# Two mixture-of-experts FFNs: blocks of 32 rows on four 32-column tiles in place of blocks of 64 on two

## The reference

```
x   = layernorm(h)
p   = softmax of the two largest of (x @ gate)
y_e = (silu(x @ W1_e) * (x @ W3_e)) @ W2_e        # hidden width 512 in the first FFN, 1024 in the second
out = h + sum over the two chosen experts of p_e * y_e
```

## Time and profile before

| | |
|---|---|
| median of 3 runs | 972.81 us (970.16 to 972.89) |
| profiled execution | 968.8 us, its span 967.1 us |
| busy over the span | PE 802.5, PEld 461.0, DVE 477.5, ACT 407.9, POOL 219.5 us |
| granted TensorE clock, mean | 0.894 |
| router and steps of the first FFN | about 384 to 548 us of the span |
| router and steps of the second FFN | about 673 to 951 us |

### The profile page before, as it was taken

How to read it: one execution, slowest core, us unless ns; L and a number is a source line. 1 busy time by engine, 2 the same in 40 slices (tenths; PEclk the granted TensorE clock), 3 DMA queues, 4 the chain that set the end, 5 groups by cost and what they waited for, 6 DMA issues and landing times. The chain is left out here.

```text
span 967.1 us, 15054 instructions
## 1 busy us (share of the span) xinstructions
PE 802.5 (83%) x4860; PEld 461.0 (48%) x4861; DVE 477.5 (49%) x1186; ACT 407.9 (42%) x589; POOL 219.5 (23%) x276
## 2 busy tenths in 40 slices
PE   3859548899997897499999397886599999999993
PEld 1857426533663455454444164554444444444441
DVE  4975443399767672733333367563622222222332
ACT  4133125543244555244555043444255555555541
POOL 1051000277020100123343121332112222222110
PEclk8579757999989999699999798799599999999996
DMA  3000055000034320611111334870603103700004
GB/s 115 1 0 1 0 175 228 1 0 1 1 97 128 101 56 3 230 34 43 43 43 33 104 111 142 241 219 4 234 12 122 53 22 128 308 22 22 25 12 136
DMA packets 52953, 78.62 MB, mean 81 GB/s; under 512 B 9796, under 2 KB 45764, under 8 KB 49700
## 3 DMA queue, kind: packets, MB, share of 16 engines
q1 hardware_dynamic: 48040, 67.37, 21.2%
q0 software_dynamic: 4864, 10.63, 3.6%
HBM read 54.77 MB, written 10.49 MB: 67 GB/s over the span
## 5 line engine op out<-in xcount | busy, mean ns | idle before, releaser
L2195 PE MATMUL psum<-ring,f_x_t 128*64 x480 | 218.8, 598 | 1.2 <-DVE f_x_t L1971 1.2
L2197 PE MATMUL psum<-f_w_up,f_x_t 128*64 128x512 f32 x480 | 218.8, 598 | 0.0
L2073 ACT ACTIVATE f_w_up<-ring 128x1024 f32 x120 | 125.7, 1050 | 44.0 <-issue 44.0
L2195 PEld LDWEIGHTS psum<-ring,f_x_t 128*64 128x64 f32 x480 | 60.8, 136 | 114.3 <-issue 114.3
L2213 PE MATMUL psum<-ring,f_gated_t 128*64 x480 | 113.5, 379 | 1.7 <-issue 1.7
L1966 DVE TENSOR_TENSOR f_gated<-f_silu,psum 128x512 f32<-128x512 f32 x60 | 41.2, 687 | 148.9 <-PE psum L2197 148.9
L2215 PE MATMUL psum<-f_w_down,f_gated_t 128*64 128x256 f32 x480 | 113.5, 379 | 0.0
L2056 ACT ACTIVATE f_gated_t<-psum 128x512 f32<-128x512 f32 x60 | 35.8, 597 | 140.0 <-PE psum L2204 140.0
L2213 PEld LDWEIGHTS psum<-ring,f_gated_t 128*64 128x64 f32 x480 | 65.6, 137 | 61.3 <-issue 35.3
L1983 DVE COPY f_w_down<-ring 128x1024 f32 x60 | 42.1, 701 | 48.0 <-PE psum L2215 23.1
L2215 PEld LDWEIGHTS psum<-f_w_down,f_gated_t 128*64 128x64 f32 x480 | 65.6, 137 | 0.0
(11 more groups left out here) (297 smaller groups left out, 1422.9 us busy)
## 6 DMA issues: line engine op xcount, KB each, us to landing
ring<-in_f_experts SPq DMA_DIRECT2D x24, 1536.0 KB, 7.3
a_stack_q<-a_parts SPq DMA_DIRECT2D x96, 64.0 KB, 2.0
a_stack_k<-a_parts SPq DMA_DIRECT2D x96, 64.0 KB, 2.0
rows_in<-h SPq DMA_DIRECT2D x4, 1024.0 KB, 12.7
ring<-rows_out SPq DMA_DIRECT2D x8, 512.0 KB, 5.4
ring<-in_a_wqkv SPq DMA_DIRECT2D x2, 768.0 KB, 4.4
x_in<-in_x SPq DMA_DIRECT2D x1, 1024.0 KB, 4.8
out<-x SPq DMA_DIRECT2D x4, 256.0 KB, 2.1
```

The lines of the kernel that those rows point to most:

```text
L2073: act.activation(w_up[:, b, CT * CHUNK * side:CT * CHUNK * (side + 1)], k.ring[:, bass.ds(at + start, CT * CHUNK)], ACT.Copy).then_inc(s_w ...
L2195: pe.matmul(psum[0:HALF, 2 * b + side, :], x_t[:, xb, t, 0:HALF], k.ring[:, bass.ds(at + (CHUNK_COLS * c + start), CHUNK)], start=(t == 0) ...
L2197: last = pe.matmul(psum[HALF:P, 2 * b + side, :], x_t[:, xb, t, HALF:P], w_up[:, b, start:start + CHUNK], start=(t == 0), stop=(t == CT - 1))
```

## The change

An expert now owns blocks of 32 rows, and a step works on four of them, on four tiles of 32 columns. MAXBLK becomes 18. The first tile still reads `ring`; the other three read copies. VectorE copies the up weights of tiles 1 and 2 (2048 columns each, one instruction) and the down weights of tile 1; ScalarE copies the up weights of tile 3 and the down weights of tiles 2 and 3. The copies for tile 3 lie in `x1` and `h`, which are free by then. The engines' lists are written anew around these copies, and VectorE and ScalarE load ring columns for two tiles at once (`ring_columns`). `over`, `in_block` and `past` become views of `w_down`, and the router's constants are widened. The core of the diff:

```diff
-HALF = P // 2
-MAXBLK = ((2 * TOK + E * (HALF - 1)) // HALF + 1) // 2
+QUARTER = P // 4
+MAXBLK = ((2 * TOK + E * (QUARTER - 1)) // QUARTER + 3) // 4
...
-        past = sb("past", [P, 2 * PAIRED, E])
-        expert = sb("expert", [P, 3, 2 * PAIRED])
-        table = sb("table", [P, 2, PAIRED, 2], I32)
-        w_up = sb("w_up", [P, 2, 2 * CT * CHUNK])
-        w_down = sb("w_down", [P, 2, CHUNK // P * C])
+        expert = sb("expert", [P, 3, 4 * PAIRED])
+        table = sb("table", [P, 2, PAIRED, 4], I32)
+        own_up = sb("w_up", [P, 4, 2 * CT * CHUNK])
+        w_up = {(1, 0): own_up[:, 0], (1, 1): own_up[:, 1], (2, 0): own_up[:, 2], (2, 1): own_up[:, 3],
+                (3, 0): k.x1[:].rearrange("p t b n -> p (t b n)"), (3, 1): k.h[:].rearrange("p t b n -> p (t b n)")}
+        w_down = sb("w_down", [P, 3, 2, CHUNK // P * C])
...
 # VectorE
+            def copy_up(j, at, c, tile, b):
+
+                if chunks == 2 and tile == 1:
+                    loads = dve.value_load(table[0:1, 1, bass.ds(j, 1), 3:4], min_val=16, max_val=16 * E)
+                    dve.wait_ge(s_loaded[c], loads)
+                    dve.wait_ge(s_table, 1)
+                dve.tensor_copy(w_up[tile, b], k.ring[:, bass.ds(at[tile - 1] + CHUNK_COLS * c, 2 * CT * CHUNK)]).then_inc(s_uv, 1)
...
             dve.wait_ge(s_table, 1)
-            for c in range(chunks):
-                copy_down(0, c, c)
+            if chunks == 1:
+                dve.wait_ge(s_loaded[0], 16 * E)
+            at = ring_columns(0)
+            copy_up(0, at, 0, 1, 0)
+            copy_up(0, at, 0, 2, 0)
             take_x(0, 0)
-            gate(0, 0)
-            take_x(1, 1)
...
+            else:
+                ahead = ring_columns(1)
+                copy_up(1, ahead, 0, 1, 1)
+                take_x(1, 1)
+                copy_up(1, ahead, 0, 2, 1)
+                copy_down(0, at, 0, 0)
+                gate(0, 0)
 
-            def block_step(i, odd, more=True):
+            def block_step(i, odd, at, more=True):
                 j = 2 * i + (1 if odd else 2)
+                ahead = None
                 if chunks == 2:
-                    copy_down(j, 0, 0)
+                    copy_up(j, at, 1, 1, 1)
+                    copy_up(j, at, 1, 2, 1)
+                    copy_down(j, at, 0, 0)
                     gate(2 * j, 0)
                     take_y(j - 1, 1 - odd, 16 * i)
                     if more:
+                        ahead = ring_columns(j + 1)
+                        copy_up(j + 1, ahead, 0, 1, 0)
                         take_x(j + 1, 1 - odd)
-                    copy_down(j, 1, 1)
+                        copy_up(j + 1, ahead, 0, 2, 0)
+                    copy_down(j, at, 1, 1)
                     gate(2 * j + 1, 1)
                 else:
                     if more:
+                        ahead = ring_columns(j + 1)
+                        copy_up(j + 1, ahead, 0, 1, 1 - odd)
                         take_x(j + 1, 1 - odd)
-                    copy_down(j, 0, odd)
+                        copy_up(j + 1, ahead, 0, 2, 1 - odd)
+                    copy_down(j, at, 0, odd)
                     gate(j, odd)
                     take_y(j - 1, 1 - odd, 16 * i)
...
 # ScalarE, the same in both block_steps: take_gated, copy_up of tile 3, silu_of, copy_down
+            def copy_down(j, at, c, b):
...
+                for tile in (2, 3):
+                    act.activation(w_down[:, tile - 1, b, :],
+                                   k.ring[:, bass.ds(at[tile - 2] + (CHUNK_COLS * c + 2 * CT * CHUNK), CHUNK // P * C)],
+                                   ACT.Copy).then_inc(s_da, 1)
...
 # TensorE
             def up(q, xb, b, at, c):
+                pe.wait_ge(s_uv, 2 * q + 2)
+                pe.wait_ge(s_ua, q + 1)
+                pe.wait_ge(s_table, 1)
                 for side in range(2):
-                    pe.wait_ge(s_wu, 2 * q + side + 1)
                     for t in range(CT):
                         start = CHUNK * (CT * side + t)
-                        pe.matmul(psum[0:HALF, 2 * b + side, :], x_t[:, xb, t, 0:HALF],
-                                  k.ring[:, bass.ds(at + (CHUNK_COLS * c + start), CHUNK)], start=(t == 0), stop=(t == CT - 1))
-                        last = pe.matmul(psum[HALF:P, 2 * b + side, :], x_t[:, xb, t, HALF:P],
-                                         w_up[:, b, start:start + CHUNK], start=(t == 0), stop=(t == CT - 1))
+                        first, final = t == 0, t == CT - 1
+                        pe.matmul(psum[0:QUARTER, 2 * b + side, :], x_t[:, xb, t, 0:QUARTER],
+                                  k.ring[:, bass.ds(at + (CHUNK_COLS * c + start), CHUNK)], start=first, stop=final,
+                                  tile_position=(0, 0))
+                        for tile in range(1, 4):
+                            rows = slice(QUARTER * tile, QUARTER * tile + QUARTER)
+                            last = pe.matmul(psum[rows, 2 * b + side, :], x_t[:, xb, t, rows],
+                                             w_up[tile, b][:, start:start + CHUNK], start=first, stop=final,
+                                             tile_position=(0, QUARTER * tile))
                     last.then_inc(s_up, 1)
...
```

More of the change, by code:

```diff
@@ L1914, in _ @@
             dve.wait_ge(s_rank, 1)
-            step(dve.scalar_tensor_tensor(place[:], earlier_blocks[:].unsqueeze(1).broadcast_to(every), float(HALF),
+            step(dve.scalar_tensor_tensor(place[:], earlier_blocks[:].unsqueeze(1).broadcast_to(every), float(QUARTER),
                                           psum[:, 5, 0:TT * E].rearrange("p (t e) -> p t e", t=TT), ALU.mult, ALU.add))
@@ L2056, in take_gated @@
                 act.activation(gated_t[:, b, :], psum[:, G_BANK + b, :], ACT.Copy).then_inc(s_gto, 1)
-            def second_expert(j):
-                act.wait_ge(s_table, 1)
[L2061 to L2074, removed]
@@ L2076, in _, with ring_columns, copy_up @@
-            second = second_expert(0)
-            for side in range(2):
-                copy_up(second, 0, side, 0)
+            def ring_columns(j):
+                _, columns = nc.values_load_multi_w_load_instructions(
+                    table[0:1, 0, bass.ds(j, 1), 2:4], [mybir.EngineType.Activation], min_val=0,
+                    max_val=(RING_EXPERTS - 1) * chunks * CHUNK_COLS)
+                return columns
+            def copy_up(j, at, c, b):
+                if chunks == 2:
+                    loads = act.value_load(table[0:1, 1, bass.ds(j, 1), 3:4], min_val=16, max_val=16 * E)
+                    act.wait_ge(s_loaded[c], loads)
+                    act.wait_ge(s_table, 1)
+                act.activation(w_up[3, b], k.ring[:, bass.ds(at[1] + CHUNK_COLS * c, 2 * CT * CHUNK)], ACT.Copy).then_inc(s_ua, 1)
@@ L2079, in _ @@
+            act.wait_ge(s_table, 1)
+            act.wait_ge(s_nd, 32)
             if chunks == 1:
[L2080 to L2083, removed]
+                act.wait_ge(s_loaded[0], 16 * E)
+            at = ring_columns(0)
+            copy_up(0, at, 0, 0)
             if chunks == 2:
+                copy_up(0, at, 1, 1)
+                silu_of(0, 0)
+                copy_down(0, at, 0, 0)
@@ L2085, in _, with block_step @@
                 take_gated(0, 0)
-                second = second_expert(1)
-                copy_up(second, 0, 0, 0)
+                copy_up(1, ring_columns(1), 0, 0)
                 silu_of(1, 1)
-                copy_up(second, 0, 1, 0)
-            def block_step(i, odd, more=True):
+                copy_down(0, at, 1, 1)
+            else:
+                copy_up(1, ring_columns(1), 0, 1)
+                silu_of(0, 0)
+                copy_down(0, at, 0, 0)
+            def block_step(i, odd, at, more=True):
@@ L2103, in block_step @@
                     silu_of(2 * j + 1, 1)
-                    if more:
-                        copy_up(second, 0, 1, 0)
+                    copy_down(j, at, 1, 1)
                 else:
@@ L2108, in block_step, with turn @@
                     if more:
-                        second = second_expert(j + 1)
-                        copy_up(second, 0, 0, 1 - odd)
+                        ahead = ring_columns(j + 1)
+                        copy_up(j + 1, ahead, 0, 1 - odd)
                     silu_of(j, odd)
[L2112 to L2116, removed]
+                    copy_down(j, at, 0, odd)
+                return ahead
+            def turn(i):
+                block_step(i, 0, block_step(i, 1, ring_columns(2 * i + 1)))
+            turn(0)
             with act.Fori(1, PAIRS) as i:
-                block_step(i, 1)
-                block_step(i, 0)
-            block_step(PAIRS, 1, more=False)
+                turn(i)
+            block_step(PAIRS, 1, ring_columns(2 * PAIRS + 1), more=False)
             take_gated(chunks * MAXBLK - 1, 1)
```

111 lines of the change are left out of this document (68 added, 43 removed).

## The result

The changed kernel takes **975.12 us** (median of 12 runs, 971.43 to 980.68), the kernel before beside it 970.66 (12 runs, 968.39 to 973.33). The ratio is 1.0049, 95% interval 1.0026 to 1.0073: slower by half a per cent, where 955 was forecast. The profiled execution took 976.63 us, its span 974.6 (before: 968.8 and 967.1).

A forecast was written before the change was run, and what follows sets the result against it. TensorE was taken to bound the expert stages, as steps times its time per step. The sum -36.2 + 12 + 2.1 + 2.6 + 1 + 1 = -17.5, put on the median 972.81, gave 955.3 us; range 940 to 973.

The forecast's parts named there:

- Does a step keep its length?: Expert steps: four 32-column tiles replace two of 64, each streaming its own columns; taken as no loss.
- C: Up and down products: four tiles streaming 512 columns do not hold the pace; 989 or 1025 us, chance 0.07.
- D: TensorE's loop body, nearly doubled, is fetched again at every turn; 23 us, giving 979 us, chance 0.03.
- Fewer steps: Both FFNs: MAXBLK from 20 to 18 saves two steps of 12.01 us and two of 6.11, -36.2 us.
- The turn: TensorE's sequencer at loop turns and entry: branch and ring-column loads outlast queued matmuls; 6.0 us per FFN, +12 for both.
- VectorE's odd chunk: Second FFN: VectorE's queued copies make the gate 0 to 0.3 us late; +1 us over 18 steps.
- The queue ahead of the branch: TensorE's queue holds 16 to 18 matmuls, about four groups of down, covering 1.0 to 1.2 us instead of 2.5.
- Rival A: TensorE's loop turns: no stall, the queue stays far enough ahead; 943 us, chance 0.21.
- The first FFN: First FFN: later gate(0) at its start +2.6 us, TensorE's turns +6.0; VectorE's 4.7 us fit the 6.1 us step.
- B: VectorE's odd chunk in the second FFN, or GpSimd in the first, decides; 966 us, chance 0.14.
- Router: Router before both FFNs: longer block lists (`past` 320 to 576 elements, `over` 128 to 256) cost +2.1 us for both.
- E: Like the forecast, but several small terms at their ends, within 0.3% of before; 972 us, chance 0.05.

The follow-up runs named there:

- e1: Changed kernel with the second FFN's experts (weights and gate columns) stored in another order on the host: 951.53 us, ratio 0.9815 to the kernel before.
- e7: Kernel before the change, with only the same reordering of the second FFN's experts as e1: 971.06 us, ratio 1.0012.
- e5: Changed kernel with the four edits of e1, e2, e3 and e4 together: 935.9 us, ratio 0.9647 to the kernel before.
- e2: Changed kernel with TensorE's loop over pairs of steps written out in both FFNs: 972.42 us, ratio 1.0033 to the kernel before.
- e3: Changed kernel with VectorE's take_y moved later, behind reading ring columns (first FFN: also the first copy; first pair written out): 969.68 us, ratio 0.9999 to before.
- e4: Changed kernel with VectorE's take_x(1) moved behind the second copy, down copy and gate(0) at the first FFN's start: 973.8 us, ratio 1.004 to before.
- e9: e5 with VectorE's and ScalarE's loops over pairs of steps written out as well: 932.88 us, ratio 0.9636 to the kernel before.

## Why the prediction was wrong

**The step that failed** is "Does a step keep its length?". It asked only for the rate of four tiles and took "no loss" for the whole step. No term of the sum held the ring's refill: the size of the blocks moves an expert's last use and the next one's first use against the steps, while a place comes free only with the last down product. In its place the runs showed two stops of 10.7 us and the low clock behind them, 23.8 us in all (e1, with e7 as the control). A sign that the prediction had named, a step longer than 12.4 us, was there: one chunk alone took 16.52. It was no rival either, and the chance of 0.10 for slower stood on C and D alone, which were both wrong.

The miss is 975.12 - 955.3 = 19.8 us. The refill alone is 23.8. The 4 us the other way are two: the sum was put on a median of 3 runs, 972.81, where 12 runs gave 970.66, and the other terms together came out about 2 us below their forecast.

The other terms, from the stages of before, after and e5:

- *Fewer steps*, -36.2: right. e5 shows -12.4 and -24.5, together -36.8, in the two stages.
- *Four tiles hold the pace*: right. Up groups at 0.43 and down groups at 0.21 us, chunks of 6.10 and 5.88 us where 6.12 and 5.90 stood. The Trainium skill ("TensorE: Matmul & The Clock Gate", Measured speedup vs the span model) has 2.38x for three tiles; here four tiles of 32 columns lose nothing against two of 64; no run has one tile alone, so the ratio was not tested.
- *The turn*, +6.0 in the second FFN, and VectorE's odd chunk, +1: the sum is near, the split is not. The stage was 30.2 over e5's; less 23.8, 6.4 are left for both. TensorE's turn alone is worth 3.0 of them (e2) and take_y's place alone 1.2 (e3), because VectorE is late right behind TensorE. In the working for the odd chunk take_y's own 0.42 us was left out: its list adds up to 6.5 us and not 6.1, so the gate ends at 848.2 after the overlap, 0.1 us behind the 848.07 it was held against; measured was a gap of 0.56 for 0.31.
- *The queue ahead of the branch*: 20 matmuls, forecast from 16 to 18. With a weight load for each these are 40 places. The Trainium skill ("Advanced Engine Details and Errata", Engine Queue Depths) gives 64; that depth was not seen. Rival A is out.
- *The first FFN*: 10.7 over e5's. The start was +2.4 (e4), forecast 2.6. The steps were +8.3, forecast +6.0, and for another reason: with TensorE's turn gone nothing was won (e2), since every second step then took 7.27 us instead of 6.10, seven times 1.17. I had added VectorE's work there (4.7 of 6.1 us) and left out that it begins when the down product ends and that VectorE then stands idle to load columns, for 0.5 to 0.7 us or 2.8 at its turn. TensorE's turn counts only when VectorE's is out of the way: 0.57 us at each of seven then (e3), 4.0. So B's mechanism was at work, in the FFN that I had called free of it.
- *Copies*: 1.23 on VectorE for 1.25, 1.91 on ScalarE for 1.96. GpSimd held its cover: with it unchanged, e5's steps are 6.10 us.
- *Clock*, +1 at the first FFN's start: not seen there in the changed kernel (transposes of 0.66 us after the gap), but seen in e3 (1.7 us) and behind the stops (4.0, counted above).
- *Router*, +2.1: `past` on 576 elements took 0.759 us, 0.27 more, as worked out; the whole moved by +1.6 and -0.9 us, so the term can't be told from the spread.
- *Slips that changed nothing*: D was priced for seven turns, 23 us, where each of the two FFNs has seven. E's 972 lies inside the range of 940 to 973 that was said to leave it out.

Terms as measured: -36.8 + 23.8 + 6.4 + 8.3 + 2.4 = +4.1, and the medians differ by 4.5. That the terms add up to the change of the two stages is so by the way they were taken; what the 4.5 adds is that the rest of the program moved little.

## What to carry to other kernels

When work is cut into other pieces, write down for every buffer that is filled again in which step it is last read and in which it is next wanted, with the real sizes, and compare the time between with what the transfer takes; a margin that no wait shows is a margin of unknown size, and here it was about 1 us, by the estimate above. Where several engines are late in turn, one edit gives little until the last is made, so test the edits together as well as alone. And count an engine's chain from the event that lets it start, with its register loads, not as a sum of busy time.

## Hardware, as the runs showed it

- Four matmul tiles of 32 columns, float32, 512 columns streamed by each, keep the pace of two of 64: 0.43 us a group.
- An idle stretch of over 10 us of TensorE cost another 2.4 and 1.6 us behind it: the mean granted clock of the windows there is 0.75 and 0.78, and the four transposes took 1.11 us instead of 0.66. A stretch of 2.85 us cost nothing in the changed kernel's execution and 1.7 us in e3's.
- TensorE's loops written out (seven turns in each FFN) raised the instruction queue from 31 to 53 packets (e2); VectorE's and ScalarE's loops on top of that left it at 53 (e9). No step of e5 or e9 was late for it.
